# Second layer's single plain float32 matmuls in place of three half products; a bias moved to VectorE, another to the eviction

## The reference, cut to what matters

```
def _L1_attn_ref(x, gamma, w_qkv, w_out):
    xn = rms_norm(x, gamma)
    qkv = xn @ w_qkv
    ...
    q = q * scale
    sim = jnp.einsum('bhid,bhjd->bhij', q, k)
    attn = jax.nn.softmax(sim, axis=-1)
    out = jnp.einsum('bhij,bhjd->bhid', attn, v)
    ...
    return out @ w_out
...
xe = jnp.einsum('bsd,eod->bseo', u, Wr) + br      # experts
...
out = jnp.einsum('bsd,od->bso', input, w_ternary * alpha) + bias
```

## Time and profile before

| | us |
|---|---|
| median of 3 runs | 3154.27 |
| lowest, highest | 3150.88, 3159.85 |
| the profiled execution's own time | 3168.83 |
| its span, first to last instruction | 3167.0 |
| TensorE busy in the span | 2803.9 (89%) |
| VectorE, GpSimd, ScalarE busy | 2115.3, 2058.2, 1864.8 |

### The profile page before, as it was taken

One profiled execution on the slowest core, in us unless ns is written; L12 is line 12 of the kernel. 1 busy time (PEld: TensorE's weight loads), 2 busy tenths in 40 slices (PEclk: granted clock), 3 DMA queues, 4 the chain that ended last, 5 costly groups with the idle time before them and its releaser, 6 DMA issues.

```text
span 3167.0 us, 48881 instructions
## 1 busy us (share of the span) xinstructions
PE 2803.9 (89%) x14290; PEld 2132.5 (67%) x14290; DVE 2115.3 (67%) x3500; ACT 1864.8 (59%) x2685; POOL 2058.2 (65%) x1314
## 2 busy tenths in 40 slices
PE   5888668834448999999999999999999999999997
PEld 4777557723336677777777777777777777777775
DVE  6888443356766666766767667677676667667664
ACT  4555232211126777777767767777776777777674
POOL 4666330077744777777777777777777777777775
PEclk8999879955559999999999999999999999999999
DMA  3432245577751222223222222222222232232222
GB/s 120 134 122 85 87 131 181 172 219 214 211 176 44 61 50 72 60 57 77 45 72 61 60 73 50 68 54 71 54 64 73 44 77 55 62 77 47 70 56 46
DMA packets 266847, 281.05 MB, mean 89 GB/s; under 512 B 96755, under 2 KB 205555, under 8 KB 266740
## 3 DMA queue, kind: packets, MB, share of 16 engines
q1 hardware_dynamic: 254452, 246.17, 29.4%
q0 software_dynamic: 12288, 33.57, 3.4%
HBM read 129.67 MB, written 82.31 MB: 67 GB/s over the span
## 4 chain that ended last, share of the span: by engine, by line
PE 66%; ACT 1%; DVE 1%; DMA 1%; POOL 1%; issue 1%; SPq 0%; POOLq 0%; ACTq 0%; DVEq 0%
PE psV_b L1601 7%; PE psV_b L1596 7%; PE psV_b L1597 7%; PE psS_b L1584 7%; PE psS_b L1583 7%; PE psN_b L1569 7%; PE psY_b L1524 4%; PE psX_b L1524 4%; PE psY_b L1525 4%; PE psY_b L1526 4%; PE psX_b L1525 4%; PE psX_b L1526 4%; POOL pp_lo_b L1314 1%; DMA xT_lo<-xT_lo_dram 1%; PE psN_b L1653 0%
## 5 line engine op out<-in xcount | busy, mean ns | idle before, releaser
L1314 POOL TENSOR_TENSOR pp_lo_b<-pf_b,pp_hi_b 128x1024 fp32r<-128x1024 f32 x512 | 1229.8, 2402 | 609.0 <-ACT pp_hi_b L1356 522.9
L1460 DVE TENSOR_REDUCE negmax_b<-psN_b 128x2 fp32r<-128x1024 f32 x512 | 627.2, 1225 | 379.2 <-PE psN_b L1569 371.6
L1351 ACT ACTIVATE pf_b<-psS_b 128x1024 f32<-128x1024 f32 x512 | 526.1, 1028 | 239.0 <-PE psS_b L1584 235.9
L1583 PE MATMUL psS_b<-qA_b,kA_b 128*128 128x512 f32 x1024 | 405.8, 396 | 6.6 <-DVE qB_b L1475 4.7
L1584 PE MATMUL psS_b<-qB_b,kB_b 68*128 68x512 f32 x1024 | 406.5, 397 | 0.0
L1597 PE MATMUL psV_b<-pp_hi_b,vals_lo_b 128*64 128x512 f32 x1024 | 403.8, 394 | 0.0
L1596 PE MATMUL psV_b<-pp_hi_b,vals_hi_b 128*65 128x512 f32 x1024 | 402.0, 393 | 1.5
L1569 PE MATMUL psN_b<-kA_b,qA_b 128*128 128x512 f32 x1024 | 322.7, 396 | 4.7 <-DVE negmax_b L1460 4.6
L1601 PE MATMUL psV_b<-pp_lo_b,vals_hi_b 128*65 128x512 f32 x1024 | 320.2, 394 | 5.0 <-POOL pp_lo_b L1314 5.0
L1375 ACT ACTIVATE kA_b<-psX_b 64x512 fp32r<-64x512 f32 x256 | 152.1, 594 | 290.0 <-PE psX_b L1526 285.1
L1356 ACT ACTIVATE pp_hi_b<-pf_b 128x1024 fp32r<-128x1024 f32 x256 | 271.5, 1060 | 8.1
(11 more groups left out here) (243 smaller groups left out, 6123.1 us busy)
## 6 DMA issues: line engine op xcount, KB each, us to landing
kA_b<-kA_b SPq DMA_DIRECT2D x128, 256.0 KB, 3.2
qB_b<-qA_b SPq DMA_DIRECT2D x128, 256.0 KB, 2.9
inverse_b<-inverse_dram SPq DMA_DIRECT2D x256, 128.0 KB, 3.1
xs_e<-rows_dram SPq DMA_DIRECT2D x144, 128.0 KB, 2.1
results_dram<-ys_e SPq DMA_DIRECT2D x72, 256.0 KB, 2.3
x_a<-x_dram SPq DMA_DIRECT2D x16, 512.0 KB, 4.7
part_dram<-acc_a SPq DMA_DIRECT2D x32, 256.0 KB
acc_s<-part_dram SPq DMA_DIRECT2D x32, 256.0 KB
```

Source lines behind the costliest of these rows:

```text
L1314: pool.tensor_tensor(pp[1][:, c], pf[:, c], pp[0][:, c].bitcast(F32), ALU.subtract).then_inc(pl_pool, 1)
L1351: a.activation(pf[:, c], psS[:], ACT.Exp).then_inc(exp_act, 1)
L1460: v.tensor_reduce(negmax[:, n.slot(2), 2 * c:2 * c + 2], psN[:], AX.X, ALU.max, negate=True).then_inc(mx_dve, 1)
L1583: pe.matmul(psS[:, t], kA[:, s, keys], qA[:, s], start=True, stop=False)
```

## The change

In `phase_b` all operands of the four products become plain F32 tiles and each product one matmul. The tiles `pp`, the low halves, `otf` and the operations that made them are gone; `pf` gets a second slot, so that ScalarE's exponential of a head waits for the weighing two heads back. GpSimd writes `ot` directly. The weights are loaded in place and ScalarE scales those of q, k and v. Between the stages there is one transposed `xT` in DRAM instead of two halves. In `settle` the feed-forward product is one plain F32 matmul, the bias is added by VectorE, the two powers are one operation on four numbers, and `finish` stands behind the factors. In `experts` the bias is broadcast to all partitions by one DMA of 2 MB and added at the eviction, which VectorE now does for every pair, reading the offsets into registers of its own.

```diff
@@ experts, VectorE @@
-                if m >= 0 and m % 2 == 1:
+                if m >= 0:
+                    at = [v.value_load(kept.table[0:1, m * U + t:m * U + t + 1], min_val=0, max_val=(NE - 1) * D) for t in range(U)]
+                    if m == 0:
+                        v.wait_ge(br_in, 16)
                     need(v, y_pe, 1, m, 1)
...
-                    v.tensor_copy(ys[:, m % 4].rearrange("p a b -> p (a b)"), psY[:, m % 3]).then_inc(y_dve, 1)
+                    for t in range(U):
+                        v.tensor_tensor(ys[:, m % 4, t], psY[:, m % 3, t * D:(t + 1) * D], bias_bc[:, bass.ds(at[t], D)],
+                                        ALU.add).then_inc(y_dve, 1)
@@ experts, TensorE @@
-                    pe.matmul(out, kept.pick[:], brow[:, bass.ds(at, D)], start=True, stop=False)
@@ settle, TensorE @@
-                        pe.matmul(out, xrt[0][:, u % 2, t, k], kept.wtern[:, k], start=(k == 0), stop=False)
-                        mm = pe.matmul(out, xrt[1][:, u % 2, t, k], kept.wtern[:, k], start=False, stop=(k == KD - 1))
+                        mm = pe.matmul(out, xrt[:, u % 2, t, k], kept.wtern[:, k], start=(k == 0), stop=(k == KD - 1))
@@ phase_b @@
-        pf = sb("pf", [P, 2, 2, S])
-        pp = [sb(f"pp_{p}", [P, 2, 2, S], F32R) for p in ("hi", "lo")]
...
+        pf = sb("pf", [P, 2, 2, 2, S])
+        vals = sb("vals", [P, TB, H, DH + 1])
@@ phase_b, ScalarE @@
-                    after(a, pl_pool, 2, g + -1, c + 1)
-                    a.activation(pf[:, c], psS[:], ACT.Exp).then_inc(exp_act, 1)
...
+                    after(a, pv_pe, 2, g + -2, c + 1)
+                    a.activation(pf[:, g.slot(2), c], psS[:], ACT.Exp).then_inc(exp_act, 1)
@@ phase_b, TensorE @@
-                    mm = three(psX[:, 0], (wqkv[0][:, k, cols], wqkv[1][:, k, cols]),
-                               (xT[0][:, k], xT[1][:, k]), k == 0, k == KD - 1)
+                    mm = pe.matmul(psX[:, 0], wqkv[:, k, cols], xT[:, k], start=(k == 0), stop=(k == KD - 1))
...
-                after(pe, ph_dve if c else ph_act, 1, g, 1)
-                after(pe, v_dve, 8, b, TB * (h // 8) + 2 * c + 2)
+                after(pe, exp_act, 2, g, c + 1)
+                after(pe, v_act, 8, b, TB * (h // 8) + 2 * c + 2)
...
-                    pe.matmul(psV[0:DH + 1, g.slot(2)], values(0, h, i), pp[0][:, c, t], start=(i == 0), stop=False)
-                    pe.matmul(psV[0:DH, g.slot(2)], values(1, h, i), pp[0][:, c, t], start=False, stop=False)
-                after(pe, pl_pool, 2, g, c + 1)
-                for t in range(2):
-                    i = 2 * c + t
-                    mm = pe.matmul(psV[0:DH + 1, g.slot(2)], values(0, h, i), pp[1][:, c, t], start=False, stop=(i == TB - 1))
+                    mm = pe.matmul(psV[0:DH + 1, g.slot(2)], vals[:, i, h], pf[:, g.slot(2), c, t], start=(i == 0), stop=(i == TB - 1))
...
-                            mm = three(psY[:, 0, 0:D], (ot[0][:, q, rows], ot[1][:, q, rows]),
-                                       (wout[0][:, q], wout[1][:, q]), q == 4 * half, q == 4 * half + 3)
+                            mm = pe.matmul(psY[:, 0, 0:D], ot[:, q, rows], wout[:, q], start=(q == 4 * half), stop=(q == 4 * half + 3))
```

More of the change, by code:

```diff
@@ L860, in _ @@
                         right = [part[:, k, bass.ds(at, D)] for part in wr]
-                        pe.matmul(out, left[0], right[0], start=False, stop=False)
+                        pe.matmul(out, left[0], right[0], start=(k == 0), stop=False)
                         pe.matmul(out, left[0], right[1], start=False, stop=False)
@@ L864, in _, with settle @@
                 mm.then_inc(y_pe, 1)
-def settle(nc, io, results, part, xT_hi, xT_lo, base_dram, early, kept):
+def settle(nc, io, results, part, xT_dram, base_dram, early, kept):
     NU = part.shape[0]
@@ L893, in settle @@
         xr = sb("xr", [P, 2, U, D])
-        xrt = [sb(f"xrt_{p}", [P, 2, U, KD, P], F32R) for p in ("hi", "lo")]
+        xrt = sb("xrt", [P, 2, U, KD, P])
         base = sb("base", [P, 2, U, D])
@@ L1393, in step @@
                     after(a, pv_pe, 2, m, 2)
[L1394 removed]
+                    after(a, ot_pool, 1, q + -2, 1)
+                    if q.reg is None and q.const == 0:
+                        a.wait_ge(w_act, KD)
                     a.activation(inverse[other, r], psV[total, m.slot(2)], ACT.Copy).then_inc(nm_act, 1)
@@ L1521, in _, with loaded @@
         def _(pe):
-            def three(out, left, right, start, stop):
-                (lh, ll), (rh, rl) = left, right
-                pe.matmul(out, lh, rh, start=start, stop=False)
-                pe.matmul(out, lh, rl, start=False, stop=False)
-                return pe.matmul(out, ll, rh, start=False, stop=stop)
             pe.wait_ge(ready, READY)
             pe.wait_ge(const_dve, 2)
-            def split(c):
-                pe.wait_ge(w_dve, KD * (c + 1))
-            def values(part, h, t):
-                return vals[part][:, t, h]
+            def loaded(c):
+                if c < SCALED:
+                    pe.wait_ge(w_act, KD * (c + 1))
+                else:
+                    pe.wait_ge(w_in[c], 16)
             def kq(g, p, which):
@@ L1543, in kq @@
                 if p.reg is None and p.const in (0, HP // 2):
-                    split(which if p.const == 0 else 4 + which)
+                    loaded(which if p.const == 0 else 4 + which)
                 b = Step(p.reg, 1, p.const // HP)
                 if which == 0:
-                    after(pe, xt_in, 32, b, 32)
+                    after(pe, xt_in, 16, b, 16)
                     after(pe, kq_dve, 4, p + -1, 4)
@@ L1609, in shared @@
                         k, fb, n = former(g)
-                        after(pe, v_dve if k == "V" else o_dve, 8, fb, n + 1)
+                        after(pe, v_act if k == "V" else o_dve, 8, fb, n + 1)
                     rows = slice(t * P, (t + 1) * P)
                     if b.reg is None and b.const == 0 and t == 0:
-                        split({"V": 2, "O": 6}[kind] + half)
+                        loaded({"V": 2, "O": 6}[kind] + half)
                     if kind == "V":
-                        after(pe, xt_in, 32, b, 32)
+                        after(pe, xt_in, 16, b, 16)
                         cols = slice(2 * H * DH + half * S, 2 * H * DH + (half + 1) * S)
                         for k in range(KD):
-                            mm = three(psY[:, 0], (xT[0][:, k, rows], xT[1][:, k, rows]),
-                                       (wqkv[0][:, k, cols], wqkv[1][:, k, cols]), k == 0, k == KD - 1)
+                            mm = pe.matmul(psY[:, 0], xT[:, k, rows], wqkv[:, k, cols], start=(k == 0), stop=(k == KD - 1))
                         mm.then_inc(v_pe, 1)
@@ L1682, in two_layers @@
                 experts(nc, io, rows, results, region, jobs, kept, raw, raw_in)
-            settle(nc, io, results, part, xT_hi, xT_lo, base, early, kept)
-        phase_b(nc, io, xT_hi, xT_lo, base, early)
+            settle(nc, io, results, part, xT, base, early, kept)
+        phase_b(nc, io, xT, base, early)
 def lay_out(i):
```

268 lines of the change are left out of this document (83 added, 185 removed).

## The result

The changed kernel takes 3411.15 us (median of 4 runs, 3410.01 to 3416.83), the kernel before beside it 3156.93. The ratio is 1.081, 95% interval 1.079 to 1.083: slower by 254 us, where 292 were forecast. The time lies in the predicted range, 35 us under the value.

A forecast was written before the change was run, and what follows sets the result against it. The prediction took TensorE to bound the attention stage, 2.2 ms of 3.17. Attention +356, settle -44, experts -15 and attention's start and end -5 made +292 us, taking the median of 3154.27 to 3446 us, range 3384 to 3520.

The forecast's parts named there:

- The bound and the count: Attention loop: TensorE sets the pace; 8 products a step go from 0.696 to 0.87 us each, +356 us.
- a step isn't 9.8 to 10.0 us: Attention loop: sign that the prediction is wrong; the per-head matmul was expected every 9.9 us.
- the named bounds: Attention, plain product of 512 columns: 0.853 us without overhead to 0.928 at F32R's pace, +322 to +475 us.
- Attention's start and end: Outside the attention loop: -1 us for dropped weight splits, -4 for vanished `pp_lo` waits; together -5, from -12 to +5.
- Settle: Settling stage: a unit goes from 8.60 to 7.1 us, -44 us in all; at worst nothing, at best -50.
- Experts: Experts stage: -10 us in the pairs, -5 at the start; together -15, from -30 to +25.
- the bad case: Experts: a VectorE register load of 0.6 us instead of 0.3 makes a pair 3.3 us; the range's end, +25.
- The attention term: Attention loop: 8 products a step, each 0.87 instead of 0.696 us, 1.39 us a step over 256 steps, +356 us.
- long products at F32R's pace: Rival 1, attention: a plain product of 512 columns takes 0.928 us, total 3565 us; chance 0.08.
- both side stages without gain: Part of rival 2: neither `settle` nor `experts` gets shorter, total put at 3530 us; rival's chance 0.12.
- one record of two passes: Rival 3, attention: a product of 512 columns takes 0.435 us, step 6.4 us, total 2556 us; chance 0.03.
- Rival 2: `settle` and `experts` give nothing: either alone puts the time at about 3490 us, both at 3530; chance 0.12.

The follow-up runs named there:

- the two runs of them alone: Kernel before with only the changed experts stage: 0.9985, -5 us; kernel before with only the settling stage's new order, halves kept: 0.9874, -40 us.
- the run saves 462: Changed kernel with each plain weighing matmul replaced by a single F32R matmul, low halves left out: 2951.8 us, 0.9332 of the kernel before.
- the kernel with halves: Kernel before with only settle's order changed (bias on VectorE, one power on four numbers, base sum behind the factors), transposed rows still in halves: 0.9874, -40 us.

## Why the prediction was right, and where it missed

*The bound and the count: right.* Two records a product (2048 on the weighing's line), TensorE at 100% and clock 1.00, GpSimd almost idle, the per-head matmul every 9.74 us where 9.9 was named. The prediction called itself wrong if a step isn't 9.8 to 10.0 us; by that sign this term failed, though narrowly, and it is the one that was mis-sized. The product is 0.857 us, not the 0.87 taken from line 706's rows of 256 columns: 8 x 0.013 x 256 = 27 us. Half of the 0.013 is reading: in the trace's nanoseconds the two products of line 706 take 0.863 us from end to end, not the 0.87 that the rounded rows gave. The other half is the doubling: records of 256 columns are 0.216 us apart and those of 512 columns 0.429, a little less than twice. The remaining 14 us of the term are the gaps: a step rebuilds as 12 x 0.232 + 8 x 0.857 = 9.64 us, which leaves 0.10 us for the small matmul and gaps where 0.15 was kept. Both ends of the named bounds held, 0.853 and 0.928. The rule of the Trainium skill on the fixed cost per matmul (TensorE: Matmul & The Clock Gate, section "Wait — 56ns, not 53.3ns?") gave 0.858 us and +332 us, and this trace agrees with it to 0.001 us. It would have been the better choice for the plain type, and it still misses F32R, 0.232 where it says 0.216. The Trainium skill's halved rate for FP32_LOW_HIGH (Perfetto Trace Analysis, Engine Utilization) holds for one record and not for the product, as the prediction read it.

*Attention's start and end: the step that failed.* It said -1 for the start (-6 to +5) and -4 for the end. From the last unit's first sum in `settle` to the first scores into `psS` this pair of profiles has -11.3. It is a wide pair: the distance is 47.4 to 51.2 us in the six profiles with weights split into halves (48.6 on average) and 39.9 to 43.5 in the eight with plain ones (41.1), -7.5, which is still outside the range. In the chain of the kernel before that ends with the first scores, VectorE's weight splits stand several times:

```profile
936.08 1.43 DVE wqkv_lo_b L1435 x2
944.82 2.66 DVE wqkv_lo_b L1435 x4
956.98 1.23 DVE wout_lo_b L1440
```

The lower clock, which the prediction set against them, shows little: in the two chains six F32R records take 2.90 us there (948.94 to 951.84) and four plain ones 2.70 (from 879.92). That the splits are the cause is read from the chain; no run moved them alone. The -4 for the end can't be read from this pair (35.5 and 36.2 us from the last per-head matmul on); over all profiles it is 35.0 to 39.8 us with halves and 30.8 to 36.6 with plain weights, 4 to 5 us less on average.

*Settle: right, -44 against -43.2, with luck in the parts.* A unit of 7.14 us where 7.1 was worked out; its chain in one unit, which answers to the earlier trace rows:

```profile
761.23 0.25 DVE L1006 BATCH_NORM_AGGREGATE mv_s<-stats_s 128x2 f32<-128x6 f32 x2
761.39 0.66 DVE L1007 TENSOR_TENSOR x1b_s<-x_s,fbias_bc_s 128x512 f32<-128x512 f32 x1
...
761.56 0.55 POOL L951 TENSOR_TENSOR vs_s<-mv_s,eps_s 128x4 f32<-128x4 f32 x1 [0.32 <-DVE mv_s L1006]
762.19 1.03 POOL L953 TENSOR_TENSOR root_s<-vs_s,power_s 128x4 f32<-128x4 f32 x1
763.26 0.16 DVE L1011 TENSOR_TENSOR fac_s<-root_s 128x2 f32<-128x2 f32 x1 [1.20 <-POOL root_s L953]
...
764.26 0.88 DVE L979 SCALAR_TENSOR_TENSOR base_s<-psF_s,fac_s,x1b_s 128x256 f32<-128x256 f32 x2
```

The wait for the power is 1.20 us, not 0.7, as GpSimd's small sum took 0.55 us and not the 0.20 that was taken from before, so from the end of the statistics to the first factor it is 1.78 us where 1.36 was reckoned. The small factor operations gave 0.31 of it back: 1.00 us (763.26 to 764.26) where 1.31 was taken. Two misses that had nothing to do with each other cancelled. `psF` is waited for only in the last unit; its chain from the factors on took 4.5 to 6.8 us, where 6.6 of the 7.1 had been reckoned.

*Experts: right in its sign, too large.* -15 was said, -10 of it in the pairs and -5 at the start; it is -11.3 in this pair of profiles and about -8 over all of them. The start came as said (20.8 to 16.0 us from the first weight copy to the first eviction), the pairs did not: 2.89 us where 2.85 was named, from 2.99 in this pair of profiles, and over all profiles 0.05 us a pair, 3 us in all, where 10 were taken. A register load on VectorE took 0.31 us, not the 0.6 of the bad case.

*The sum.* 314 - 43 - 11 - 11 = 249 us, and 254 by the medians, against 292. The attention term came out 42 us under its 356, while the side terms make -66 where -64 was said. The two profiles alone say 241, since the profiled run of before was 12 us over its median, 8 of them in the first stage. The rivals: long products at F32R's pace (0.928 us) is refuted by the rows, both side stages without gain by the two runs of them alone, one record of two passes by the count. Rival 2's times hold more than its name: 3490 for the experts alone and 3530 for both take the experts' loss of 25 us, while no gain there would be 3461 and 3505.

## What to carry to other kernels

Count TensorE's passes before changing a number type: a plain float32 product was two records of two passes, 0.857 us for 512 columns, against 0.696 for three F32R products, so dropping the halves made the code simpler and the bounding engine 23% slower on them. What the other engines were freed of was worth nothing in the stage in which TensorE is busy all the time. And take a bundle apart: two of its three parts gained 49 us together, and the third lost 303, six times as much, so the time of the whole said nothing of them. And when the count of passes says that a shorter row saves 640 us and the run saves 462, look at the distance between the ends of TensorE's records at each place of a step: it shows the waits in full, where the idle rows show about half.

## What was not expected of the hardware

- A pass of 512 columns took 0.232 us in F32R, and 0.214 to 0.216 in bfloat16 and in plain float32.
- GpSimd's sum of 128x4 numbers took 0.55 us beside VectorE's bias sum out of SBUF alone, and 0.19 us in the kernel with halves, beside VectorE's subtraction that reads PSUM:

```profile
763.46 0.19 POOL L973 TENSOR_TENSOR vs_s<-mv_s,eps_s 128x4 f32<-128x4 f32 x1 [1.06 <-DVE mv_s L1037]
```

  That the neighbour's operands are the cause is only argued; no run changed them alone.
- ScalarE stood for 7 to 9 us twice near the end of the first stage in the profiles of some sittings and not in those of others, with the same instructions: 8 us of 3160, near the 9 us that a measurement of this kernel can tell.
